# A two-layer adaLN network: layer 1's attention output product for two tiles at a time, transposed, from rounded terms

## The reference

```
Q = relu(x @ Wq + bq); K = relu(x @ Wk + bk); V = x @ Wv + bv
S_cos += (K cos) V^T;  S_sin += (K sin) V^T;  z_cos += K cos;  z_sin += K sin
out = (Q cos . S_cos + Q sin . S_sin) / max(Q cos . z_cos + Q sin . z_sin, 1e-6)
y = out @ Wo + bo
x = x + ga * y
```

## Time and profile before

| what | value |
|---|---|
| median of 3 runs | 861.15 us (859.77 to 862.86) |
| span of the profiled execution (the page gives no other time of it) | 860.6 us |
| PE busy | 798.8 us, 93% |
| DVE busy | 611.5 us, 71% |
| ACT busy | 434.6 us, 50% |
| POOL busy | 394.6 us, 46% |
| output products, L1716, in the chain that ended last | 6% |
| mean granted clock of TensorE | 0.966 |

### The profile page before, as it was taken

One profiled execution on the slowest core, in us unless ns is written; L12 is line 12 of the kernel. 1 busy time (PEld: TensorE's weight loads), 2 busy tenths in 40 slices (PEclk: granted clock), 3 DMA queues, 4 the chain that ended last, 5 costly groups with the idle time before them and its releaser, 6 DMA issues.

```text
span 860.6 us, 32362 instructions
## 1 busy us (share of the span) xinstructions
PE 798.8 (93%) x13678; PEld 695.9 (81%) x13678; DVE 611.5 (71%) x1776; ACT 434.6 (50%) x944; POOL 394.6 (46%) x399
## 2 busy tenths in 40 slices
PE   6999984489998799999999999999999999999998
PEld 5777764489997678888889888889888888878887
DVE  7897785357773676676677776787877778757865
ACT  6555533244542665656546566566574645523322
POOL 4357685604544473554645754556643533500000
PEclk9999996599998999999999999999999999999999
DMA  9824000163421200000010000100000000038661
GB/s 294 259 67 161 27 29 13 41 184 102 135 86 45 83 27 4 3 28 4 15 40 4 28 4 3 53 4 4 4 3 3 5 3 3 4 79 148 143 126 39
DMA packets 67904, 49.65 MB, mean 58 GB/s; under 512 B 5322, under 2 KB 62778, under 8 KB 67377
## 3 DMA queue, kind: packets, MB, share of 16 engines
q1 hardware_dynamic: 64288, 42.41, 18.4%
q0 software_dynamic: 3328, 5.16, 1.8%
q10 hardware_dynamic: 144, 0.02, 0.0%
HBM read 33.20 MB, written 16.10 MB: 57 GB/s over the span
## 4 chain that ended last, share of the span: by engine, by line
PE 72%; issue 13%; DVE 6%; DMA 3%; ACT 2%; another core or an unknown queue 1%; SPq 1%; POOL 1%; PEldq 0%; PEld 0%; DVEq 0%; ACTq 0%; POOLq 0%
PE psum L1560 11%; PE psum L1665 7%; PE psum L1716 6%; PE psum L1690 6%; PE psum L1244 6%; PE psum L2349 5%; PE psum L1595 5%; PE psum L1627 5%; PE psum L2367 4%; PE psum L1705 4%; PE psum L1607 3%; PE psum L1578 3%; PE psum L1279 3%; DMA sb_e_x<-disp 1%
## 5 line engine op out<-in xcount | busy, mean ns | idle before, releaser
L1560 PE MATMUL psum<-sb_wkv,sb_a_hs 128*128 128x512 f32 x384 | 122.1, 426 | 1.3 <-ACT sb_a_hs L2036 0.7
L2248 POOL TENSOR_TENSOR sb_a_qr<-sb_h,sb_a_csq 128x512 f32<-128x512 f32 x64 | 81.0, 1288 | 92.0 <-PE psum L1690 88.1
L2248 POOL TENSOR_TENSOR sb_a_qr<-sb_a_qp,sb_a_csq 128x512 f32<-128x512 f32 (+1 forms) x64 | 72.2, 1149 | 94.6 <-PE psum L1690 94.6
L1844 ACT ACTIVATE sb_a_vr<-sb_a_va,sb_consts 128x520 f32<-128x520 f32 x128 | 86.6, 726 | 14.6 <-DVE sb_a_va L2106 14.3
L310 POOL DMA_INDIRECT disp<-sb_h,sb_slot x64 | 67.9, 1062 | 32.2 <-issue 16.9
L1560 PEld LDWEIGHTS psum<-sb_wkv,sb_a_hs 128*128 128x128 f32 x384 | 63.6, 190 | 13.5 <-issue 1.2
L1183 POOL DMA_INDIRECT chosen<-sb_m_h3t,sb_e_row x40 | 39.4, 984 | 69.3 <-ACTq L1357 49.2
L1665 PE MATMUL psum<-sb_a_mid,sb_a_qr 64*64 64x65 f32 x2048 | 70.9, 218 | 0.0
L1244 PE MATMUL psum<-sb_e_xt,sb_e_ws 128*128 128x320 f32 x384 | 65.5, 327 | 5.4 <-issue 4.3
L1690 PE MATMUL psum<-sb_a_vr,sb_a_kb 64*64 64x130 f32 x1920 | 70.1, 272 | 0.0
L1244 PEld LDWEIGHTS psum<-sb_e_xt,sb_e_ws 128*128 128x128 f32 x384 | 59.6, 198 | 9.2 <-issue 5.2
(11 more groups left out here) (289 smaller groups left out, 1986.2 us busy)
## 6 DMA issues: line engine op xcount, KB each, us to landing
sb_h<-turned SPq DMA_DIRECT2D x32, 256.0 KB, 5.5
sb_e_w<-in_w SPq DMA_DIRECT2D x24, 256.0 KB
chosen<-sb_empty SPq DMA_DIRECT2D x8, 512.0 KB, 6.1
sb_a_g<-chosen SPq DMA_DIRECT2D x12, 256.0 KB, 3.1
disp<-sb_empty SPq DMA_DIRECT2D x4, 650.0 KB, 9.9
sb_e_x<-disp SPq DMA_DIRECT2D x7, 325.0 KB
sb_a_wo<-in_wo SPq DMA_DIRECT2D x4, 512.0 KB, 4.5
out<-sb_x SPq DMA_DIRECT2D x7, 256.0 KB, 3.9
```

The costliest lines, as they stand in the source:

```text
L1560: ins = pe.matmul(self.values_bank(i) if kv else self.bank[0], hs[:, part, at:at + P], self.Wkv[ws][:, h, w], start=(k == 0), stop=(k == 2))
L1844: ins = act.activation(self.Vr[i % 2][:, :, k, :], self.Va[i % 3][:], ACT.Copy, scale=self.c[("cos1", "sin1")[k]][:, n:n + 1])
L2248: ins = g.tensor_tensor(self.Qr[i % 2][:, k, :, t], qp, rows(self.csQ[:, k, c * P + t.start:(c + 1) * P], PH), ALU.mult)
```

## The change

1. The output product is made for a pair of tiles p, transposed: Wo, split into high and low parts, stands still, the turned outputs of two tiles (256 columns) move: 8 x 3 fp32r matmuls. The halves of 64 are swapped by the order in which the moving operand is read. It is done in steps 4p+5 for p < 15, the last one behind the steps.
2. ACT multiplies the result (128 x 256, channels in rows) by the gate's column (`output_gated1`); in step 4p+6 PE turns it back with two transposes (`output_returned`), and DVE adds both tiles to x in one operation. The result lies in bank 4, columns 0 to 255, and for the last pair in bank 1.
3. The outputs of a step are copied once, 128x512 (`outputs_scalar`), to one of two fp32 homes; ACT rounds them to the high part after the keys' copy and cut (`outputs_high`); POOL makes the low part one step later (`outputs_low`, in step i for step i-2).
4. POOL's `mix` is spread: two operations at i%8 = 0, one each at 1, 2 and 3. The bias is added at i%8 = 1. The third norm's statistics move on DVE from i%8 = 2 to 3 and its roots on POOL from 3 to 4.
5. Wo is loaded once, in fp32, with the other weights at the start (in layer 0's attention), and split in expert 5; the four `load_wo` and four `gate_out` go.
6. Behind the steps the last output product, its addition, the last norm's statistics and tiles, and the routing of group 6 stand later in the lists.
7. Buffers are laid over others, and the ring memory for POOL's DMAs is 8192 bytes a partition.

The diff, cut to its core:

```diff
+    OUTPUT_AT = {4 * p + 5: p for p in range(PAIRS1 - 1)}
+    RETURN_AT = {4 * p + 6: p for p in range(PAIRS1 - 1)}
...
-        for m in range(HD // P):
-            ins = pe.matmul(self.output_home(n), self.oT1[m // PH][n % 2][:, m % PH, :], self.Wog[b % 2][:, m, :], start=(m == 0),
-                            stop=(m == HD // P - 1))
+        pe.wait_ge(S["c_OTc"], 8 * p + 8)
+        for k, (ws, part) in enumerate(((0, 0), (1, 0), (0, 1))):
+            if part:
+                pe.wait_ge(S["c_OTl"], 4 * p + 4)
+            for m in range(HD // P):
+                turned = self.oT1[part][:, m, :].rearrange("p (n r t) -> p n r t", n=2, r=2)
+                if m // 2 % 2:
+                    turned = turned[:, :, ::-1, :]
+                ins = pe.matmul(out.rearrange("p (n r t) -> p n r t", n=2, r=2), self.Wo[ws][:, m, :], turned,
+                                start=(k == 0 and m == 0), stop=(k == 2 and m == HD // P - 1))
         ins.then_inc(S["c_Y"], 1)
+    def output_returned(self, p):
+        pe, S, at = self.pe, self.S, 2 * P if p == self.PAIRS1 - 1 else 0
+        pe.wait_ge(S["c_y"], p + 1)
+        for t in range(2):
+            ins = pe.transpose(self.output_home(p)[:, at + t * P:at + (t + 1) * P], self.y[:, t * P:(t + 1) * P],
+                               self.c["ident"])
+        ins.then_inc(S["c_yT"], 1)
...
-        act.copy(out[:, 0:2, :], got[:, 0:2, :])
-        act.copy(out[:, 2:4, 0:DH], got[:, 2:4, DH:P])
-        act.copy(out[:, 2:4, DH:P], got[:, 2:4, 0:DH]).then_inc(S["c_OTc"], 1)
+        act.wait_ge(S["c_OTl"], max(0, i - 1))
+        act.copy(self.oTf[i % 2].rearrange("p m t -> p (m t)"), self.bank[3]).then_inc(S["c_OTc"], 1)
+    def outputs_high(self, i):
+        act, S = self.act, self.S
+        act.wait_ge(S["c_Y"], i // 4)
+        act.wait_ge(S["c_OTc"], 2 * i + 1)
+        act.copy(self.outputs_place(0, i), self.oTf[i % 2]).then_inc(S["c_OTc"], 1)
+    def output_gated1(self, p):
+        act, S, b = self.act, self.S, p // (TB // 2)
+        act.wait_ge(S["c_Y"], p + 1)
+        act.wait_ge(S["c_yT"], p)
+        act.activation(self.y, self.output_home(p)[:, 0:2 * P], ACT.Copy, scale=self.mT[1][:, 2, b:b + 1]
+                       ).then_inc(S["c_y"], 1)
+    def outputs_low(self, i):
+        g, S = self.pool, self.S
+        g.wait_ge(S["c_OTc"], 2 * i + 2)
+        g.tensor_tensor(self.outputs_place(1, i), self.oTf[i % 2], self.outputs_place(0, i).bitcast(F32), ALU.subtract
+                        ).then_inc(S["c_OTl"], 1)
...
         pe.wait_ge(S["c_state"], 2 * i + 2)
         if i in self.OUTPUT_AT:
-            pe.wait_ge(S["c_x"], self.OUTPUT_AT[i] + 1)
+            pe.wait_ge(S["c_y"], self.OUTPUT_AT[i] + 1)
+        if i in self.RETURN_AT:
+            pe.wait_ge(S["c_x"], self.RETURN_AT[i] + 1)
... l1_gpsimd, one step
             if known(i + 1):
                 self.queries_gpsimd(i + 1)
-            if known(i) and i % 8 == 0 and i // 8 + 2 < NGRP:
-                self.mix(g, i // 8 + 2)
-            if i % 8 == 3 and i >= 8:
+            if known(i - 2):
+                self.outputs_low(i - 2)
+            if i % 8 == 0 and i // 8 + 2 < NGRP:
+                mixed = self.mix_parts(g, i // 8 + 2)
+            if i % 8 < 4:
+                next(mixed, None)
+            if i % 8 == 0:
+                next(mixed, None)
+            if i % 8 == 4 and i >= 8:
                 self.roots(i // 8 - 1, self.rt3, "3")
... moe_tensor
-        self.output1_tensor(NT - 1)
         self.gate_up_tensor(1, 1)
         self.gate_up_tensor(1, 2)
+        self.output1_tensor(self.PAIRS1 - 1)
         self.gate_up_tensor(1, 3)
+        self.output_returned(self.PAIRS1 - 1)
         self.down_tensor(0)
-        self.tiles_turned(self.xn1, "c_xn3", NGRP - 1, [("c_x", NT), ("c_lg", NGRP - 1)])
         self.gate_up_tensor(1, 4)
... moe_vector
-        self.output1_vector(NT - 1)
-        some(self.stats_parts(NGRP - 1, self.st3, "3", ("c_x", NT)), 30)
         self.hidden_vector(1, 1)
...
         self.hidden_vector(1, 3)
-        some(self.weights1_parts(NGRP - 2), 30)
+        self.output1_vector(self.PAIRS1 - 1)
+        some(self.stats_parts(NGRP - 1, self.st3, "3", ("c_x", self.PAIRS1)), 30)
         self.split_vector(2)
...
         self.hidden_vector(1, 4)
+        some(self.weights1_parts(NGRP - 2), 30)
         self.weight_vector(1, 3)
```

More of the change, by code:

```diff
@@ L622, in gates_wide @@
         act.wait_ge(S["mod_B"], 2 * lay)
[L623 removed]
+        act.copy(self.gateB[:], self.gate_column(lay).unsqueeze(3).to_broadcast([P, 2, B, P])).then_inc(S["mod_wide"], 1)
     def gates_kept(self, lay):
@@ L1367, in split_at @@
     def split_at(self, e, n):
-        return range(2 * e - 2, 2 * e) if 1 <= e <= 4 and n == 3 else ()
+        return range(2 * e - 2, 2 * e) if 1 <= e <= 5 and n == 3 else ()
     def l1_split(self):
@@ L1379, in l1_split @@
                     pieces.append((parts[0][:, i, cols], raw[:, i, cols], parts[1][:, i, cols]))
+        high, low = (w[:].rearrange("p (h m) d -> p h (m d)", h=2) for w in self.Wo)
+        for h in range(2):
+            pieces.append((high[:, h, :], self.raw_o[:, h, :], low[:, h, :]))
         return pieces
@@ L1465, in l1_weights @@
         self.Wq = [sb(f"a_wq{k}", [P, 2, HD // 2], F32R) for k in range(2)]
-        self.Wog = [sb(f"a_wo{k}", [P, HD // P, D]) for k in range(2)]
+        self.Wo = [sb(f"a_wo{k}", [P, HD // P, D], F32R) for k in range(2)]
         self.csQ = sb("a_csq", [P, 2, T])
@@ L1500, in l1_buffers @@
         self.O = sb("a_o", [P, 2, PH, DH])
-        halves = sb("a_ot", [P, HD // P, P])
-        spare = self.h3T[:, (NT - G4) * P:].rearrange("p (m t) -> p m t", t=P)
-        self.oT1 = [[halves[:, 0:PH, :], spare], [halves[:, PH:, :]] * 2]
+        self.oT1 = [sb(f"a_ot{k}", [P, HD // P, 2 * P], F32R) for k in range(2)]
+        self.oTf = [sb("a_otf", [P, PH, P])[:], self.gate[1, 2][:]]
         self.hT1 = sb("a_ht", [P, G4 * P])
@@ L1629, in scores_tensor, with output_home @@
         ins.then_inc(S["c_S"], 1)
-    OUTPUT_AT = {2 * n + 3: n for n in range(NT - 1)}
+    PAIRS1 = NT // 2
+    OUTPUT_AT = {4 * p + 5: p for p in range(PAIRS1 - 1)}
+    RETURN_AT = {4 * p + 6: p for p in range(PAIRS1 - 1)}
     LOGITS_AT = {8 * m + 15: m for m in range(NGRP - 1)}
-    def output_home(self, n):
-        return self.bank[1][:, 0:D] if n == NT - 1 else self.bank[4][:, 512 - D:512]
+    def output_home(self, p):
+        return self.bank[1] if p == self.PAIRS1 - 1 else self.bank[4]
     def logits_home(self, m):
@@ L2152, in outputs_vector, with output1_vector @@
                         ).then_inc(S["c_On"], 1)
[L2154 to L2159, removed]
+    def output1_vector(self, p):
+        v, S, at = self.dve, self.S, 2 * P if p == self.PAIRS1 - 1 else 0
+        x = self.X[:, 2 * p:2 * p + 2, :]
+        v.wait_ge(S["c_yT"], p + 1)
+        v.wait_ge(S["c_xb"], p // 2 + 1)
+        v.tensor_tensor(x, self.output_home(p)[:, at:at + 2 * P].rearrange("p (n d) -> p n d", n=2), x, ALU.add
+                        ).then_inc(S["c_x"], 1)
     def logits_vector(self, m):
@@ L2194, in l1_vector @@
         for i in range(steps):
-            if i >= 8 and i % 8 == 2:
+            if i >= 8 and i % 8 == 3:
                 some(parts, 30)
-                parts = self.stats_parts(i // 8 - 1, self.st3, "3", ("c_x", 4 * (i // 8)))
+                parts = self.stats_parts(i // 8 - 1, self.st3, "3", ("c_x", 2 * (i // 8)))
             if i % 8 == 4 and i // 8 + 2 < NGRP:
@@ L2290, in l1_gpsimd @@
                 self.low_part(g, i // 8 + 2)
-                self.bias_added(i // 8 + 2)
-            if i in (25, 41):
-                self.gate_out((i + 7) // 16)
             if i in (52, 60):
                 self.down_gated((i - 52) // 8)
+        for i in range(steps - 2, steps):
+            self.outputs_low(i)
         self.roots(NGRP - 1, self.rt3, "3")
@@ L2396, in moe_tensor @@
         self.hidden_product(1, 0, 1)
-        self.output1_tensor(NT - 1)
-        pe.wait_ge(S["c_OTc"], steps)
         self.gate_up_tensor(1, 1)
@@ L2444, in moe_scalar @@
         self.outputs_scalar(steps - 1)
+        self.outputs_high(steps - 1)
         self.hidden_scalar(1, 1)
         self.hidden_scalar(1, 2)
+        self.output_gated1(self.PAIRS1 - 1)
         self.hidden_scalar(1, 3)
```

77 lines of the change are left out of this document (39 added, 38 removed).

## The result

The changed kernel takes **886.72 us** (median of four runs, 885.50 to 890.35), the kernel before 860.96 in the same job: 1.031 times as long, 95% interval 1.027 to 1.034. I had forecast 855.7. It is slower by 26 us where I expected 5 less.

A forecast was written before the change was run, and what follows sets the result against it. TensorE was taken as the bound, busy 93% of 860.6 us and waiting for nobody in the steps; -8.0 + 3.9 + 0.9 + 0.5 - 1.6 - 1.1 = -5.4 gave 855.7 us, range 850 to 860.5.

The forecast's parts named there:

- the 0.08 for slower: Whole kernel: chance given to a measured time slower than before by more than 2.6 us.
- Part A: Output product on PE: 57.0 us out, 49.0 in at 0.119 a matmul, -8.0 us (bounds -11.2 and +2.6).
- Part B: GpSimd every eighth step: later norm roots make PE wait 0.55 in seven groups, +3.9 us; low parts hidden.
- Part C: ACT and DVE: ACT's copies, rounding and gate cost nothing; DVE's moved statistics +0.9, scaling in step 7 +0.5 us.
- Part D: Experts: without two output-weight loads the wait for the third expert's slots goes; -1.6 us (bounds -2.3 and 0).
- Part E: Behind the steps: -3.7 at the first down product, +2.6 new idle before the second; -1.1 us.
- the 1.7 that I had named and left out: Behind the steps: +1.7 us on top if PE's clock falls again after the idle before the second down product.
- GpSimd and VectorE blocking each other: Rival, steps 3 and 4: GpSimd's added operations stretch VectorE's, +15 us at most, 867 us; chance 0.06.
- The dearer product: Rival, output product: 0.147 us a matmul, so +2.6 in place of -8.0, 866 us; chance 0.03.
- Of the rivals, 1: Moved waits in steps and behind them have cover, only work goes: -13.3 us, 847.8 us; chance 0.20.
- the -9.3 of its half: The rival of covered waits with half of the stalls kept: 851.8 us.

The follow-up runs named there:

- the kernel shifted by 136: The changed kernel with 34 small matmuls (136 instructions) added once ahead of layer 1's first scores: 887.08 us, 1.031 times the kernel before.
- the two kernels with fillers: The changed kernel plus PE instructions added to move packet borders: already met waits and 15 small matmuls, 895.58 us; small matmuls only, 889.49 us.
- experiment 5: The changed kernel with each step's V product moved from ahead of the scores to between the state products and the state update: 943.92 us.
- experiment 12: The changed kernel with VectorE's routing of group 6 put back behind the last weighting of the second expert block: 885.67 us, 1.027 times the kernel before.
- experiment 4: The changed kernel with 714 already met waits on PE beside its long matmuls, and 15 small matmuls at the start: 895.58 us.

## Why the prediction was wrong, point by point

**Where it failed.** Two sentences: "in the steps PE waits for nobody, and any PE work that goes or comes there moves the end", and of the 2.1 us of "issue" only that it is "no engine". I took it for noise. It was the only sign, in the rows that I showed, of the resource that decided: a supply that just keeps up, and whose margin hangs on where the borders fall. I counted durations, and never instructions. Work that went left stalls behind, 31.6 us. None of my rivals had it; the 0.08 for slower was on other mechanisms.

**Part A** held in its mechanism and was mis-sized by 1.7. The timeline of PE, steps 33 and 34, which have no stall, and the start of step 35, answers to the earlier trace rows:

```profile
548.58 0.96 PE L1554 MATMUL psum<-sb_wkv,sb_a_hs 128*128 128x512 f32 x3
550.07 0.60 PE L1601 MATMUL psum<-sb_consts,sb_a_o 128*128 128x128 f32 x4
550.43 3.11 PE L1720 MATMUL psum<-sb_a_ot,sb_a_wo 128*128 128x256 f32 x24
553.38 0.60 PE L1572 MATMUL psum<-sb_consts,sb_a_kb 128*128 128x128 f32 x4
...
557.56 0.95 PE L1554 MATMUL psum<-sb_wkv,sb_a_hs 128*128 128x512 f32 x3
...
559.48 0.38 PE L1729 MATMUL psum<-sb_consts 128*128 128x128 f32 x2
...
563.84 0.97 PE L1554 MATMUL psum<-sb_wkv,sb_a_hs 128*128 128x512 f32 x3
```

Steps of 8.98 and 6.28 us, and 6.07 for the next (to 569.91): my 8.95, 6.3 and 6.09. A product takes 553.38 - 550.43 = 2.95, 0.123 a matmul for my 0.119; with 0.22 for the turning, 16 pairs cost 50.7 and A is -6.3, not -8.0. The cause of that 4 ns was not tried. The 109 ns for 256 columns by the formula of the Trainium skill, "TensorE: Matmul & The Clock Gate", section "Back-to-back issue gap", which the page gives for a single matmul by itself, are 14 under this row's 123.

**Part B** was mis-sized: +3.9 forecast, 0.2 in the steps' waits, and not over 1.2 in four places of the kernel shifted by 136. The quiet parts fell by 6.4, which A's share in the loop (15 pairs for 31 tiles, 55.4 down to 48.0 in the records' spacing) explains but for +1.0. So B and C together are worth 1.0, not 5.3. The low parts came in time, as I had it: GpSimd's timeline of step 34,

```profile
557.35 2.53 POOL L2283 TENSOR_TENSOR sb_a_qr<-sb_a_qp,sb_a_csq 128x512 f32<-128x512 f32 x2 [2.69 <-PE psum L1689]
559.83 1.29 POOL L2299 TENSOR_TENSOR sb_a_ot<-sb_a_otf,sb_a_ot 128x512 fp32r<-128x512 f32 x1
```

ends 3.56 us after its step's start, 3.7 forecast. Had the stalls not come, more of B might show; the two kernels with fillers, few of whose bursts stall, have 1.1 and 1.3 us of waits for ScalarE's normalised tiles.

**Part C**: no entry of the waits names the gate (L1860) in the changed kernel. In experiment 5, where the step is tighter, it is there, so the 0.1 us that I left it was real, and thin:

```profile
PE psum L1664 <- ACT sb_consts L1860: 7.8, 15, 0.5
```

**Part D**: the loop starts 2.9 us earlier, more than my 1.6 and my bound of 2.3. The third expert's slots are no longer waited for, as the row below shows; the rest was not followed, but some of it is "issue" too, 3.0 us at the experts' product (L1246) between 150 and 304 us where before had 4.3:

```profile
182.49 0.71 PE L1199 MATMUL psum<-sb_consts,sb_e_x 128*128 128x128 f32 x5
```

**Part E** was right in its parts: full clock at the first down product (granted 1.00 from 793 to 806 us), 2.74 of idle before the second (I had 2.6), and the clock fell again behind it (0.63 from 809.4 to 812, where experiment 12 has 1.00), the 1.7 that I had named and left out: 6.36 for 40 records in place of 4.73. Experiment 12 gives both back, 3.7 of 4.4. The part behind the last scores is 2.5 longer, of which 1.4 is the last product, now of a pair, which A had counted.

**The rivals.** GpSimd and VectorE blocking each other: DVE is busy for 603.2 us, 8.3 less than before, and no entry points there. The dearer product: 0.123, not 0.147. Of the rivals, 1 came nearest for everything outside the bursts: -6.8 was measured, between my -5.4 and the -9.3 of its half. That -6.8 lies so near to -5.4 is partly luck. By parts it is -6.0 for the product (-7.4 in the loop and +1.4 for the last one; I had -8.0), +1.0 for B and C (+5.3), -2.9 for the experts (-1.6) and +1.1 behind the steps (-1.1): four misses of 1.3 to 4.3 us that nearly cancel.

No kernel that I ran beats the one before. That the change would gain about 7 us with bursts as smooth as before's is worked out from the table of the parts, not run.

## What to carry to other kernels

An "issue" entry in the middle of a run of equal small matmuls was here a supply of instructions that had run out, and is a reason to look for one. Count instructions, not only time: where a stretch issues more than a packet's worth faster than a packet comes, the time depends on the number of instructions ahead of it, and a change of some dozens ahead of it can cost or give much: here 80 added instructions cost 37 us in 860, and 136 cost 49. Before a tuned kernel and its successor are compared, shift both by half a packet: a tuned kernel may be one that happens to stand well. And long matmuls between bursts are cover for that supply, so taking them out or heaping them in one step is not free.

## What the runs showed of the hardware that I had not expected

- The supply: 256 instructions a packet, a stall of 1.3 to 1.6 us on average for a badly placed burst, 1.9 to 2.3 for one that follows a stalled burst with its first border at 160 to 203.
- Instructions that hold nothing but waits already met pass PE 0.106 us apart when they stand in a row. Up to ten in a step hid beside its long matmuls (175 of them cost 2.4 us in experiment 4), 33 in a step cost 2.0 us or more (264 of them 19.9).
- A small matmul repeated on one quarter of the array costs 0.116 us; the same ones through the quarters in turn 0.030. The added matmuls in the timelines of PE, shift by 208 first (52, two records each), then by 256 (64):

```profile
303.35 6.22 PE L1624 MATMUL psum<-sb_a_qp,sb_a_kt 64*64 64x64 f32 x103
...
309.41 0.22 PE L1624 MATMUL psum<-sb_a_qp,sb_a_kt 64*64 64x64 f32 x1
```

```profile
303.39 2.10 PE L1627 MATMUL psum<-sb_a_qp,sb_a_kt 64*64 64x64 f32 x128
```
